# An LSTM recurrence between two deformable convolutions: a shorter scan, other PSUM banks, three products moved into the norm, and explicit loads of function tables

## The reference, cut to what matters

```python
def step(carry, xs):
    h, c = carry
    xi_t, xf_t, xg_t, xo_t = xs
    i_t = jax.nn.sigmoid(xi_t + h @ V_i)
    g_t = jnp.tanh(xg_t + h @ V_c)
    o_t = jax.nn.sigmoid(xo_t + h @ V_o)
    c_new = h * c + i_t * g_t
    h_new = o_t * jnp.tanh(c_new)
    return ((h_new, c_new), h_new)
```

## Time and profile before

| | us |
|---|---|
| median of 3 runs | 995.34 |
| lowest, highest | 995.21, 996.75 |
| the profiled execution | 994.94 |
| its span in the trace | 993.1 |
| norm(1), from the residual's end to the last xn | 138.97 to 147.60 |
| first scan of the recurrence, last scan | 153.94, 581.26 |
| conv(1), first product on PE | 595.20 |
| first product of the experts on PE | 729.80 |

### The profile page before, as it was taken

One profiled execution on the slowest core, in us unless ns is written; L12 is line 12 of the kernel. 1 busy time (PEld: TensorE's weight loads), 2 busy tenths in 40 slices (PEclk: granted clock), 3 DMA queues, 4 the chain that ended last, 5 costly groups with the idle time before them and its releaser, 6 DMA issues.

```text
span 993.1 us, 18107 instructions
## 1 busy us (share of the span) xinstructions
PE 770.1 (78%) x6224; PEld 571.4 (58%) x6224; DVE 557.3 (56%) x1560; ACT 556.9 (56%) x1580; POOL 369.8 (37%) x296
## 2 busy tenths in 40 slices
PE   5799976666666666666666557999869999899996
PEld 2477865555554555555555444788736666466663
DVE  3798753555445355333333336887556776567675
ACT  2667743333355355333333335677558888688884
POOL 0777720000000000000000006877348888588885
PEclk7999995555555555555555558999969999899999
DMA  9600000000001100000000000000000010100001
GB/s 222 161 2 1 2 1 1 1 1 1 1 1 75 75 1 0 1 1 1 1 0 1 1 0 1 2 1 3 1 0 2 2 76 2 77 2 1 1 2 22
DMA packets 5861, 18.54 MB, mean 19 GB/s; under 512 B 1093, under 2 KB 2822, under 8 KB 5254
## 3 DMA queue, kind: packets, MB, share of 16 engines
q1 hardware_dynamic: 5478, 17.21, 6.0%
q10 hardware_dynamic: 288, 0.13, 0.1%
HBM read 9.47 MB, written 0.52 MB: 10 GB/s over the span
## 4 chain that ended last, share of the span: by engine, by line
PE 35%; POOL 21%; DVE 15%; ACT 13%; issue 12%; DVEq 1%; SPq 1%; DMA 1%; POOLq 1%; ACTq 0%
POOL zw L813 20%; PE bank L458 10%; DVE bank L1055 6%; PE bank L460 6%; PE bank L332 5%; ACT scan_io L709 5%; PE bank L349 5%; ACT tcell L713 5%; PE bank L297 4%; DVE hr L1061 4%; DVE hid L888 1%; PE bank L319 1%; DVE dist L873 1%; PE bank L362 1%; PE bank L277 1%
## 5 line engine op out<-in xcount | busy, mean ns | idle before, releaser
L773 POOL TENSOR_TENSOR st<-tent,tentx 128x768 f32<-128x768 f32 x96 | 150.9, 1606 | 524.7 <-DVE tentx L881 511.5
L813 POOL TENSOR_TENSOR zw<-hid,zw 128x512 f16<-128x512 f32 x176 | 204.1, 1160 | 49.0 <-ACT zw L740 30.3
L458 PE MATMUL bank<-hr,lv 64*64 64x8 f32 x512 | 96.8, 261 | 158.8 <-DVE hr L1061 158.8
L458 PEld LDWEIGHTS bank<-hr,lv 64*64 64x64 f32 x512 | 72.5, 200 | 205.4 <-DVE hr L1061 205.3
L1160 DVE SCALAR_TENSOR_TENSOR hid<-bank,wsc,st 128x512 f32<-128x512 f32 x176 | 132.0, 750 | 75.6 <-ACT st L744 70.2
L709 ACT ACTIVATE scan_io<-bank 64x16 f32<-64x16 f32 x256 | 49.3, 193 | 210.7 <-PE bank L460 210.5
L1055 DVE TENSOR_TENSOR_SCAN bank<-scan_io 64x32 f32<-64x32 f32 x256 | 57.5, 225 | 163.2 <-ACT scan_io L709 163.2
L498 PE MATMUL bank<-st,wh 128*128 128x512 f16 x352 | 136.8, 389 | 11.5 <-POOL st L806 5.4
L744 ACT ACTIVATE st<-bank,wsc 128x512 f32<-128x512 f32 x176 | 121.0, 688 | 35.3 <-PE bank L499 17.6
L499 PE MATMUL bank<-st,wl 128*128 128x512 f16 x352 | 136.7, 388 | 0.0
L513 PEld LDWEIGHTS bank<-w2p,zw 128*128 128x128 f16 x1408 | 96.9, 98 | 45.3 <-POOL zw L813 4.0
(11 more groups left out here) (149 smaller groups left out, 1133.5 us busy)
## 6 DMA issues: line engine op xcount, KB each, us to landing
w13s<-w SPq DMA_DIRECT2D x8, 704.0 KB, 18.0
w2f<-w SPq DMA_DIRECT2D x4, 384.0 KB, 26.8
w13s<-wh SPq DMA_DIRECT2D x2, 704.0 KB, 3.4
w13s<-wl SPq DMA_DIRECT2D x2, 704.0 KB, 4.6
wh<-w13s SPq DMA_DIRECT2D x2, 704.0 KB, 3.9
wl<-w13s SPq DMA_DIRECT2D x2, 704.0 KB, 5.2
w2f<-w2p SPq DMA_DIRECT2D x2, 384.0 KB, 5.2
w2p<-w2f SPq DMA_DIRECT2D x2, 384.0 KB, 5.8
```

Source lines behind the costliest of these rows:

```text
L458: nc.tensor.matmul(both[:, 0, t, :], lv[:, C:2 * C], prev, start=False, stop=True, skip_group_check=True)
L773: nc.gpsimd.tensor_tensor(st[p][:, t, k:k + KG, :].rearrange("p k (y x) -> p k y x", x=16), ty, tx, ALU.mult)\
L813: nc.gpsimd.tensor_tensor(hl[:, u % MR, :], hid[:, u % MR, :], hh[:, u % MR, :], ALU.subtract)\
```

## The change

- The scan takes three elements per batch element, not four (24 and not 32), with the order of its two operations exchanged: first multiply, then add. `scan_io` has another layout, with its two operand lists 26 elements apart, and bank 7 holds 24 elements.
- The gates of a row lie in banks 3 and 4, the gate o in banks 5 and 6. The banks of the weight scales become 0 and 1.
- The three bias products of row 0 go into the `middle` hook of `norm(1)`. Their waits (weights loaded, weights scaled, `ones` set) go with them.
- The memsets of `scan_io` and of the first h stand at DVE's start. The one of the cell is gone, and with it the wait for it.
- ACT loads tables by instructions of its own: the root's at the head of each norm, the next stage's right after the root (root, tanh, sigmoid, exp), sigmoid's after the one root of `bnw`, and Silu's ahead of the expert loop.

```diff
-        scan_io = sb("scan_io", [C, 2, B, 4])
-        cell = bank[7][0:C, 0:B * 4].rearrange("p (b k) -> p b k", k=4)
+        scan_io = sb("scan_io", [C, 2 * B * 3 + 8])
+        cell = bank[7][0:C, 0:B * 3].rearrange("p (b k) -> p b k", k=3)
+        scan_add = scan_io[:, 0:24]
+        scan_mul = scan_io[:, 26:50]
+        scan_one = scan_io[:, 0:52].rearrange("p (a n) -> p a n", a=2)[:, :, 0:24] \
+            .rearrange("p a (b k) -> p a b k", k=3)[:, :, :, 1]
+        scan_ig = scan_io[:, 0:56].rearrange("p (a n) -> p a n", a=2)[:, :, 0:24] \
+            .rearrange("p a (b k) -> p a b k", k=3)[:, :, :, 0]
+        scan_hc = scan_add.rearrange("p (b k) -> p b k", k=3)[:, :, 2]
...
-            norm(1, [("c0_res", BQ)])
-            pe.wait_ge(s("ld_lstm"), 16 * 3)
-            pe.wait_ge(s("n1_xn"), 2)
-            pe.wait_ge(s("l_scaled"), 4)
-            pe.wait_ge(s("l_init"), 4)
...
-                bk, col = (bank[2 + q], 0) if gate == 2 else (bank[q], gate * 128)
+                bk, col = (bank[5 + q], 0) if gate == 2 else (bank[3 + q], gate * 128)
...
+            def biases():
+                pe.wait_ge(s("ld_lstm"), 16 * 3)
+                pe.wait_ge(s("l_init"), 3)
+                pe.wait_ge(s("l_scaled"), 4)
+                for gate in range(3):
+                    gates_x(0, 3 * gate)
+
+            norm(1, [("c0_res", BQ)], biases)
+            pe.wait_ge(s("n1_xn"), 2)
...
             for k in range(9):
-                gates_x(0, k)
+                if k % 3 > 0:
+                    gates_x(0, k)
...
-            def norm(l, eps):
-
+            def norm(l, eps, following):
+
+                nc.scalar.preload_act_table(ACT.Sqrt)
                 for j in range(2):
...
                 nc.scalar.activation(dev[:, :], bank[2][:, 0:16], ACT.Sqrt, bias=epsc[:, eps:eps + 1])\
                     .then_inc(s(f"n{l}_sd"), 1)
+                nc.scalar.preload_act_table(following)
...
-            norm(0, 0)
+            norm(0, 0, ACT.Sqrt)
             act.wait_ge(s("ld_conv"), 16 * 5)
             nc.scalar.activation(bnw[:, 0:1], bnp[:, 3:4], ACT.Sqrt, bias=epsc[:, 1:2]).then_inc(s("bn_a"), 1)
+            nc.scalar.preload_act_table(ACT.Sigmoid)
...
-            norm(1, 1)
+            norm(1, 1, ACT.Tanh)
...
-                nc.scalar.activation(scan_io[:, :, :, 2], both, ACT.Tanh).then_inc(s("l_act"), 1)
+                nc.scalar.activation(scan_ig, both, ACT.Tanh).then_inc(s("l_act"), 1)
...
-                nc.scalar.activation(tcell[:, :], cell[:, :, 3], ACT.Tanh, scale=0.5).then_inc(s("l_tc"), 1)
+                nc.scalar.activation(tcell[:, :], cell[:, :, 2], ACT.Tanh, scale=0.5).then_inc(s("l_tc"), 1)
...
-            norm(2, 0)
+            norm(2, 0, ACT.Sigmoid)
             conv(1)
...
-            norm(3, 1)
+            norm(3, 1, ACT.Exp)
...
             nc.scalar.activation(gt[:, 0, :, :], gt[:, 1, :, :], ACT.Exp).then_inc(s("m_exp"), 1)
+            nc.scalar.preload_act_table(ACT.Silu)
...
             nc.vector.memset(ones[:, :], 1.0).then_inc(s("l_init"), 1)
+            nc.vector.memset(scan_io[:, :], 0.0).then_inc(s("l_init"), 1)
+            dve.wait_ge(s("l_init"), 2)
+            nc.vector.memset(scan_one, 1.0).then_inc(s("l_init"), 1)
+            nc.vector.memset(hr[:, 2 * W - 1, :], 0.0).then_inc(s("l_h"), 1)
...
             norm(1)
-            nc.vector.memset(scan_io[:, :, :, :], 0.0).then_inc(s("l_init"), 1)
-            dve.wait_ge(s("l_init"), 2)
-            nc.vector.memset(scan_io[:, :, :, 1], 1.0).then_inc(s("l_init"), 1)
-            nc.vector.memset(scan_io[:, 1, :, 3], 1.0).then_inc(s("l_init"), 1)
-            nc.vector.memset(cell[:, :, :], 0.0).then_inc(s("l_c0"), 1)
-            nc.vector.memset(hr[:, 2 * W - 1, :], 0.0).then_inc(s("l_h"), 1)
...
                 nc.vector.tensor_tensor_scan(cell[:, :, :].rearrange("p b k -> p (b k)"),
-                                             scan_io[:, 0, :, :].rearrange("p b k -> p (b k)"),
-                                             scan_io[:, 1, :, :].rearrange("p b k -> p (b k)"), 0.0,
-                                             ALU.add, ALU.mult).then_inc(s("l_c"), 1)
+                                             scan_mul, scan_add, 0.0, ALU.mult, ALU.add).then_inc(s("l_c"), 1)
```

More of the change, by code:

```diff
@@ L446, in spread_scales @@
                 pe.wait_ge(s("w_pow"), 3)
-                nc.tensor.matmul(bank[5][:, 0:2], ones[:, :], wpow[:, 2, :], start=True, stop=True)\
+                nc.tensor.matmul(bank[1][:, 0:2], ones[:, :], wpow[:, 2, :], start=True, stop=True)\
                     .then_inc(s("w_bc"), 1)
             for k in range(9):
-                gates_x(0, k)
+                if k % 3 > 0:
+                    gates_x(0, k)
             for n in range(STEPS):
@@ L455, in _ @@
                 prev = hr[:, (n - 1) % (2 * W), :]
-                both = bank[r % 2][0:C, 0:256].rearrange("p (k b t) -> p k t b", k=2, t=W)
-                go = bank[2 + r % 2][0:C, 0:128].rearrange("p (b t) -> p t b", t=W)[:, t, :]
+                both = bank[3 + r % 2][0:C, 0:256].rearrange("p (k b t) -> p k t b", k=2, t=W)
+                go = bank[5 + r % 2][0:C, 0:128].rearrange("p (b t) -> p t b", t=W)[:, t, :]
                 nc.tensor.matmul(both[:, 0, t, :], lv[:, C:2 * C], prev, start=False, stop=True,
@@ L701, in lift @@
                                      ACT.Copy, scale=0.5).then_inc(s("l_up"), 1)
-            act.wait_ge(s("l_init"), 4)
+            act.wait_ge(s("l_init"), 3)
             for n in range(STEPS):
                 r, t = n // W, n % W
-                both = bank[r % 2][0:C, 0:256].rearrange("p (k b t) -> p k t b", k=2, t=W)[:, :, t, :]
-                go = bank[2 + r % 2][0:C, 0:128].rearrange("p (b t) -> p t b", t=W)[:, t, :]
+                both = bank[3 + r % 2][0:C, 0:256].rearrange("p (k b t) -> p k t b", k=2, t=W)[:, :, t, :]
+                go = bank[5 + r % 2][0:C, 0:128].rearrange("p (b t) -> p t b", t=W)[:, t, :]
                 act.wait_ge(s("l_gi"), n + 1)
-                nc.scalar.activation(scan_io[:, :, :, 2], both, ACT.Tanh).then_inc(s("l_act"), 1)
+                nc.scalar.activation(scan_ig, both, ACT.Tanh).then_inc(s("l_act"), 1)
                 act.wait_ge(s("l_o"), n + 1)
@@ L997, in scales @@
                 elif k == 4:
[L998 removed]
+                    power("w", wpow, bank[0], WTOP)
                 elif k == 9:
                     dve.wait_ge(s("w_bc"), 1)
[L1001 removed]
+                    nc.vector.tensor_copy(wsc[:, 2:4], bank[1][:, 0:2]).then_inc(s("w_scale"), 1)
                 elif k == 10:
[L1003 removed]
+                    nc.vector.reciprocal(wsc[:, 0:2], bank[1][:, 0:2]).then_inc(s("w_scale"), 1)
                 elif k == 11:
@@ L1046, in residual @@
                     .then_inc(s("l_res"), 1)
-            dve.wait_ge(s("l_init"), 4)
-            dve.wait_ge(s("l_c0"), 1)
+            dve.wait_ge(s("l_init"), 3)
             for n in range(STEPS):
@@ L1064, in _ @@
                     dve.wait_ge(s("l_h"), n + 2)
-                    nc.vector.scalar_tensor_tensor(out=scan_io[:, 0, :, 3], in0=hr[:, n % (2 * W), :], scalar=0.5,
-                                                   in1=cell[:, :, 3], op0=ALU.mult, op1=ALU.mult)\
+                    nc.vector.scalar_tensor_tensor(out=scan_hc, in0=hr[:, n % (2 * W), :], scalar=0.5,
+                                                   in1=cell[:, :, 2], op0=ALU.mult, op1=ALU.mult)\
                         .then_inc(s("l_hc"), 1)
```

4 lines of the change are left out of this document (2 added, 2 removed).

## The result

The changed kernel took 981.6 us (978.6 to 984.6, 4 runs) beside 996.1 for the kernel before (995.2 to 999.3). The ratio is 0.9852, with a 95% interval of 0.9821 to 0.9883. Forecast was 986.0 with a range of 983.8 to 989.2, so the direction was right and the gain was larger than the range allowed. Two later series of the same kernel gave 0.9878 (0.9841 to 0.9914) and 0.9892 (0.9874 to 0.9911). Over all 13 runs the median is 983.4, and single runs lie between 978.6 and 986.6. So the true gain is nearer 12 us than 14, and still above the forecast's 9.3. By the four runs of the result the range is missed by 2.2 us, by the median of all 13 by only 0.4.

The account below looks back on a forecast made before the run. The recurrence was taken to be bound by its serial 1.66 us round, with no engine full. Terms 4.8 + 3.6 + 0.8 + 0.1 = 9.3 us off the 995.34 median gave 986.0, range 983.8 to 989.2 (8 in 10).

Parts of the forecast that it names:

- the starts of the convolutions: Start of conv(0) and conv(1): sigmoid's load moved ahead gains 0.4 us each, 0.8 together (bounds 0 and 1.3).
- the entrance: Before the recurrence: root load 0.13, memsets 0.35, bias products 1.85, tanh load 1.30; 3.6 us together.
- norm(3): Same pattern as norm(1): the root's table loaded ahead gains 0.13 us.
- Loads that cost nothing before: Loads in norm(0), norm(2) and the expert loop's second pass: engines waited anyway, so nothing to gain.
- the clock as a rival: PE's clock changes at other moments: 984.8 us if high in norm(1), 10%; 987.5 if rising later in conv(1) or experts, 6%.
- The scan: Recurrence, 32 to 24 elements: 18.6 ns a step at 2.33 ns an element, 4.8 us over 256 steps (bounds 2.1, 5.6).
- a gain was excluded: New scan layout, exchanged operations and new banks in the recurrence: set at nothing, with only a loss thought possible.
- Exp's load: Router: exp comes 1.1 us earlier, but DVE still waits for POOL's second subtraction; counted 0 (bound 1.1).
- The table load's price: A function-table load on ACT costs 1.30 us by the trace, not the 2.66 of the skill's added drain.
- The scan did not stream at 1.05 ns: Rival in the recurrence: scan streams at 1.05 ns an element with a large fixed part, gives 2.1, time 988.7 us; 12%.
- exp's load gained nothing: Rival in the router: exp's early load gains its 1.1 us, time 984.9 us; 6%.
- the layout made nothing slower: Rival in the recurrence: 12-byte element steps cost an extra access, 0.06 us a step, 15.4 in all, time 1001.4 us; 4%.

Follow-up runs that it names:

- experiment 7: Kernel before with one explicit load, the root's, ahead of norm(0): 994.1 us, ratio 0.9985.
- experiment 8: Changed kernel with the router's weights transferred last, on a semaphore of their own, run in two series: 981.4 us (ratio 0.9867) and 978.6 (0.9840).
- Experiment 3: Kernel before with only the three-element scan and its layout: 989.9 us, ratio 0.9955.
- experiment 4: Kernel before with only the explicit loads of function tables: 992.3 us, ratio 0.9971.
- experiment 10: Changed kernel without exp's early load, which the compiler puts ahead of exp: 984.1 us.
- 11: Changed kernel with two idle PE products behind each recurrence step that carries no input products: 1013.6 us.
- 12: Changed kernel with three idle PE products behind the free recurrence steps and one behind those with input products: 1105.5 us.
- experiment 6: Changed kernel without the two explicit root loads in norm(0), which the compiler puts back where they were: 982.9 us.
- experiment 5: Kernel before with only the other gate banks, bias products in norm(1) and memsets at the start: 992.5 us, ratio 0.9972.

## Why the prediction was wrong, point by point

- **In sum** the forecast had 9.3 us, and the traces have 13.7: norm(0) 1.2 for nothing, the starts of the convolutions 2.6 for 0.8, the recurrence 5.9 for 4.8, the entrance 3.9 for 3.6, norm(3) 0.1 for 0.1. Two steps failed: norm(0), put at nothing (next point), and the size of the starts (the point after it).
- **"Loads that cost nothing before"** is the step that failed. It read from one trace that DVE takes the root only at 15.1 because of its reduction, and counted norm(0) at nothing. The reduction was indeed the last to end in that trace, where the clock was high from 8.7 to 12.1 us, over the first twelve of the 16 variance products. In the second trace of before the transfer landed at least 2.8 us earlier, and the root, behind two open loads and slow variances, held everything to the same 15.2 us. With the root's load alone ahead, conv(0) starts 1.1 us earlier (experiment 7), in after 0.7 to 1.7 us. The row of 1.28 us for the very first load, just in front of the squares, was in the trace, and it was not costed.
- **The convolutions' starts** are the largest miss. They were taken at 0.4 each, with 0.6 as the value for the first image's tents. From PE's first product to GpSimd's first, conv(0) gained 1.6 us and conv(1) 1.0. Two things account for it: sigmoid's load, and how long PE's first products run at the low clock.

```profile
20.70:25.80 5.10, 5.10 (x12) 1.83 (x12) 1.00 (x2) 0.68 (x2) 0.00 (x0) 0.50 1.01 212
```

```profile
19.10:21.90 2.80, 2.79 (x7) 1.17 (x8) 1.01 (x2) 0.70 (x2) 0.00 (x0) 1.00 1.04 225
```

  In the first trace of before (first window) all twelve products of conv(0)'s first image ran at the low level, 0.43 us each. In the first trace of after (second window) it was seven, and the clock rose at 21.8. The 1.00 printed there is again that of a stretch ahead of the first record. All traces together, in us after PE's first product of the convolution:

| | the clock rises | GpSimd's first product |
|---|---|---|
| conv(0), sigmoid's load open: both traces of before | 5.1, 5.1 | 9.90, 9.93 |
| conv(0), load ahead: experiment 8, first series | 5.1 | 9.33 |
| conv(0), load ahead: three traces of after | 2.7, 2.8, 3.7 | 8.10, 8.17, 8.62 |
| conv(1), load open: both traces of before | 3.9, 4.0 | 9.32, 9.37 |
| conv(1), load open: experiments 7 and 3 | 2.8, 2.9 | 8.77, 8.84 |
| conv(1), load ahead: three traces of after | 3.0, 3.1, 3.3 | 8.26, 8.34, 8.40 |

  At the same rise the load gives 0.6 us, and each microsecond by which the clock rises earlier, among the first image's products, gives 0.5. So the load gave 0.6 at each convolution, and the clock the other 1.0 at conv(0) and 0.4 at conv(1). That the clock rose so early is in part luck. The instructions of norm(0) and conv(0) are those of after in four more traces (experiments 4, 10, 11 and 12), and there the clock rose 3.1 to 5.8 us after the first product. Over these seven traces the stage up to GpSimd's last add ends at 136.2 us on the mean, 2.2 and not 2.8 us before the four traces with the old loads in it (138.4).

  The stretch from GpSimd's first product to its last add is no part of the gain: it took 107.6 to 107.7 us in all five traces compared. In other traces it took 105.7, 106.7 or 109.1, with the same instructions. Windows over it, the shortest and the longest (from experiment 6 and from the second run of experiment 8). In the first the clock did not fall again, in the second it fell for 6.8 us:

```profile
28.81:134.50 105.69, 98.19 (x1043) 80.96 (x1042) 86.17 (x132) 72.92 (x162) 77.55 (x51) 1.00 0.11 31
```

```profile
27.66:136.75 109.09, 100.75 (x1043) 81.94 (x1042) 86.48 (x132) 73.02 (x162) 77.53 (x51) 0.97 0.11 31
```

  The forecast had the clock as a rival, but at other places, and at 6 and 10%.
- **The scan** was mis-sized a little, and a term was missing. The scan went from 225 to 207 ns, 18 of the forecast's 18.6, so 2.2 ns an element, under the rows' estimate of 2.33. It is nearer to the 2.1 that follows from the half throughput which the Trainium skill states ("DVE: opcode table, instruction layouts, handler registers and perf-mode slots", section "Datapath and trigger behaviour"). Missing were the 6 ns on ACT's instruction. The text set the new layout at nothing and wrote that a gain was excluded, since nothing was left out. Experiment 3 shows the gain. Together 22 ns by the mean of the undisturbed rounds (1.667 to 1.645 us), 5.6 us. The other 0.3 of the 5.9 is one round of 2.0 us less, 6 and not 7 (see experiment 5).
- **The entrance** was right in its four pieces: tables 1.3 (experiment 4), products and memsets 2.5 against 2.2 (experiment 5), where the input products in one piece gave 0.3 more. The products were hidden at 2.4 GHz: 0.86 us, against 0.93 forecast by halving.
- **Exp's load, norm(2), norm(3)** came as forecast: nothing, nothing, 0.13. Silu's load was not tested alone; the expert loop took 257.7 us in the first trace of after and 257.6 in that of before.
- **The table load's price** is 1.30 us where it stands open, in experiment 5 too (149.98 to 151.28). The further 1380 ns of drain that the Trainium skill ("ScalarE: Activation LUTs", section "What ACT_TABLE_LOAD costs") adds appears in no trace here.
- **The rivals.** The scan did not stream at 1.05 ns; exp's load gained nothing; the layout made nothing slower, it gained.
- **The range** was built of the bounds of known terms and left out what the clock and the transfer do from run to run. The last stage alone scatters by 2.4 us in the traces of either kernel, and the first by 1.6 in those of after. Windows over the experts' second pass, first trace of before and second:

```profile
862.80:993.10 130.30, 120.61 (x1058) 76.65 (x1056) 85.32 (x156) 104.74 (x175) 102.08 (x88) 0.97 0.03 6
```

```profile
863.40:995.70 132.30, 122.08 (x1057) 78.06 (x1056) 85.39 (x156) 104.05 (x174) 101.94 (x88) 0.95 0.03 6
```

  That nearly every term also erred on the same side did the rest.

What stays open: whether the change itself makes the clock rise earlier in conv(0). In the four traces with the old loads it rose 4.8 to 5.1 us after the first product, in the seven with the loads of after 2.7 to 5.8, 4.0 on the mean. Why the clock stays at 1.2 GHz under a full PE is open too, and so is what makes single rounds of the recurrence late.

## What to carry to other kernels

A stage whose end is set by two chains of equal length shows only one of them in a trace: before a load is counted as free, ask when the other chain would have ended under the other clock or an earlier transfer, and take a second trace. Three traces can agree by luck as well: before a stage's gain is put down to the change, compare traces in which the clock did the same. In a serial recurrence count each element and also the layout that each instruction writes, since every nanosecond comes back once per step. Loads of function tables belong where their engine waits anyway, but only those help whose successor isn't held by something else: here those of tanh, root and sigmoid did, and those of exp and Silu did not.

## What the runs showed of the hardware that was not expected

- PE busy for 300 of 300 us, with products of 64x64 by 8 and 128x128 by 128 in fp32, had a granted clock of 0.50 throughout.
- An ACT instruction of 64x16 elements took 193 ns writing at a step of four elements and 187 at a step of three.
- Six input products in one piece took 1.54 us, and 0.62 for each two between bias products.
- Where PE's first products of a convolution start at the low clock, each microsecond by which it rises later made GpSimd's first product 0.5 us later, in traces whose rise lay 2.7 to 5.1 us behind the first product.
- In the trace of experiment 10 the clock fell for a moment in norm(1): the entrance took 13.3 us and not 11.9. The window over its first part, with a granted clock of 0.56:

```profile
136.34:140.20 3.86, 3.09 (x4) 1.17 (x4) 0.69 (x1) 1.47 (x2) 2.84 (x5) 0.56 0.00 0
```
